# Layer kernel on one core: the SBUF buffers are declared in another order

## The chip, the cores and the metric

One core of a Trainium2 chip (trn2) runs the whole program. The metric is the device time of one execution in microseconds; a lower one is better. The profile is of a separate execution, with its own time.

## The reference, cut to what matters

The input x has 8 batches of 2048 rows of 256 numbers, all float32. For every row:

```python
xn = layernorm(x)                                  # no gain, no offset
q, k, v = split(xn @ Wqkv + bqkv)                  # 256 each
qp, kp = elu(q) + 1, elu(k) + 1
kv   = einsum('bsd,bse->bde', kp, v)               # per batch, over 2048 rows
attn = (qp @ kv) / (qp . sum(kp) + 1e-6)
z    = layer_norm(xn + attn) * g1 + b1
ffn  = (silu(z @ Wg + bg) * (z @ Wu + bu)) @ Wd + bd    # 682 hidden
s    = layer_norm(z + ffn) * g2 + b2
out  = x + s * silu(xn @ (ternary(weight) * scale).T)
```

## The kernel before, in words

The rows are cut into 32 groups of 512 (`GROUPS`, `TOK`), four groups to a batch. One iteration of the main loop works on several groups at once: the norm and keys of a group some steps ahead, the attention of the next one, the feed-forward part of the present one, the last norm of the one behind. In which order each engine takes its steps is written out by hand: `TENSOR_JOBS`, `SCALAR_STEPS`, `VECTOR_STEPS`, `GPSIMD_STEPS` for the steady iterations, `FILL_...` for the first and `END_...` for the last one. The engines meet at semaphores only.

Nearly all matmuls work on pairs of float32r parts. A factor is split into a high part (rounded, by ScalarE) and a low part (the rest, by VectorE), and `products` (L1271 holds the one call of `eng.matmul`) adds high·high, low·high and high·low. In a group of the profile the moving operand stands first and the stationary one second: `bank<-wk_h,xT_h` moves `wk_h` past a stationary tile of `xT_h`. The jobs by name, with their operands (moving, then stationary) and the columns moved:

- `G`, `U`, `GU`: gate and up projection, moving zT_h or zT_l, stationary wgu_h or wgu_l, 512 columns, 66 matmuls in an iteration
- `D`: down projection, moving wd_h or wd_l, stationary h_h, h_l or ht, 256 columns, 64 in an iteration
- `K`: keys, moving wk_h or wk_l, stationary xT_h or xT_l, 256 columns, 24
- `B`: the ternary product, moving tern, stationary xT_h or xT_l, 256 columns, 16
- `N`: numerators (and, in a 257th column, denominators), moving kv_h or kv_l, stationary qp_h or qp_l, 258 columns, 24
- `XK`: attention sums, keys times rows, moving kp_h or kp_l, stationary xn_h or xn_l, 256 columns, 24 (the first four groups use unsplit kp and xn or xq)
- `Q`: queries, moving xT_h or xT_l, stationary wq_h or wq_l, 512 columns, 12
- `KV`: once in a batch, moving wv_h or wv_l, stationary xk (which lies in kv_h and kv_l), 256 columns, 12

In program order every matmul is preceded by the load of its stationary tile, 128 columns, which the profile shows as LDWEIGHTS on its own row (PEld), beside the matmul before it.

Where a buffer lies is set by the order of the `sb(...)` calls in `build_kernel` and by nothing else: each buffer takes its bytes per partition, rounded up to 32, and the next one begins behind it. From the declared shapes this gives the places below (bytes in a partition, modulo 256), and from them how far the moving operand's place lies past the stationary one's. Columns, chunks and ring slots step by multiples of 256 bytes, except in kv_h, kv_l, qp_h and qp_l, where the second chunk lies 32 bytes further (their rows of 264 and 520 numbers); the difference is the same for both chunks.

| buffer | before | after |
|---|---|---|
| wd_h, wd_l | 32 | 160 |
| h_h, h_l, ht | 96 | 96 |
| kp_h, kp_l | 0 | 160 |
| xn_h, xn_l | 96 | 96 |
| wk_h, wk_l, tern | 64 | 224 |
| xT_h, xT_l, wq_h, wq_l | 96 | 96 |
| kv_h, kv_l | 32 | 224 |
| qp_h, qp_l | 96 | 96 |
| zT_h, zT_l, wgu_h, wgu_l | 96 | 96 |
| wv_h, wv_l | 96 | 192 |

| job | moving less stationary, before | after |
|---|---|---|
| G, U, GU, Q | 0 | 0 |
| D | 192 | 64 |
| XK | 160 | 64 |
| K, B | 224 | 128 |
| N | 192 | 128 |
| KV | 64, and 32 for its second chunk | 224, and 192 |

Of the kernel before, what the change touches and what calls it, by code (L numbers as in the profile page):

```python
# [30 lines left out]
P = 128  # L31
D = 256
DC = D // P
H = 682
HF = H // P
HT = H - HF * P
HC = HF + 1
# [6 lines left out]
TOK = 512  # L44
TILES = TOK // P
# [6 lines left out]
SHIFT = 8  # L52
# [9 lines left out]
LN0 = LEAD + 1  # L62
# [150 lines left out]
def build_kernel(nc, x, wqkv, bqkv, wg, bg, wu, bu, wd, bd, g1, b1, g2, b2, wt, out):  # L213
    f32, f32r = mybir.dt.float32, mybir.dt.float32r
# [9 lines left out]
    with ctx:  # L224
        def sb(name, shape, dt=f32):
            return ctx.enter_context(nc.sbuf_tensor(name, shape, dt))
# [2 lines left out]
            return ctx.enter_context(nc.semaphore(name))  # L229


        ident = sb("ident", [P, P])
        consts = sb("consts", [P, 4])
        masks = sb("masks", [P, 2])
        norm1 = sb("norm1", [P, 2, TILES])
        norm2 = sb("norm2", [P, 2, TILES])
        kp_h = sb("kp_h", [P, TILES, D], f32r)
        kp_l = sb("kp_l", [P, TILES, D], f32r)
        den = sb("den", [P, 2, 2])
        wd_h = sb("wd_h", [P, HC, D], f32r)  # L240
        wd_l = sb("wd_l", [P, HF, D], f32r)
        kv_h = sb("kv_h", [P, DC, D + SHIFT], f32r)
        hb = sb("hb", [P, 2 * HC])
        hb0 = sb("hb0", [P, 2 * HC])
        hb1 = sb("hb1", [P, 2 * HC])
        kv_l = sb("kv_l", [P, DC, D + SHIFT], f32r)
        ve = sb("ve", [P, 3, TILES])
        vecs = sb("vecs", [P, 5, DC])
        rstd0 = sb("rstd0", [P, LN0, TILES])
        wk_h = sb("wk_h", [P, DC, D], f32r)  # L250
        wk_l = sb("wk_l", [P, DC, D], f32r)
        tern = sb("tern", [P, DC, D], f32r)
        tscale = sb("tscale", [P, 4])
        wq_h = sb("wq_h", [P, DC, D], f32r)
        wq_l = sb("wq_l", [P, DC, D], f32r)
        xT_h = sb("xT_h", [P, XT, DC, TOK], f32r)
# [5 lines left out]
        zT_l = sb("zT_l", [P, DC, TOK], f32r)  # L262
        xn_h = sb("xn_h", [P, TILES, D], f32r)
        xn_l = sb("xn_l", [P, TILES, D], f32r)
        wv_h = sb("wv_h", [P, DC, D], f32r)
        wv_l = sb("wv_l", [P, DC, D], f32r)
        NGU = (2 * HF + 1) * P
        wgu_h = sb("wgu_h", [P, DC, NGU], f32r)
        wgu_l = sb("wgu_l", [P, DC, NGU], f32r)
        qp_h = sb("qp_h", [P, DC, TOK + SHIFT], f32r)  # L270
        nmr0 = sb("nmr0", [P, LN0, TILES])
        mv = sb("mv", [P, 3, TILES, 2])
        qp_l = sb("qp_l", [P, DC, TOK + SHIFT], f32r)
        st = sb("st", [P, 3, TILES, 6])
        bvb = sb("bvb", [P, D])
        bk1b = sb("bk1b", [P, D])
        g1b = sb("g1b", [P, D])
# [101 lines left out]

        bias_line = xq[:, 1:3, :, :].rearrange("p a t d -> p (a t d)")[0:1, 0:NGU]  # L380
        b1w = nc.dram_tensor("b1w", (NGU,), f32, kind="Internal").ap()
        turned = nc.dram_tensor("turned", (2, D, TOK), f32, kind="Internal").ap()
        z_turned = nc.dram_tensor("z_turned", (2, D, TOK), f32, kind="Internal").ap()
        ROW_PARTS = [slice(at, min(at + 512, NGU)) for at in range(0, NGU, 512)]

# [3 lines left out]
        xk_h, xk_l = kv_h[:, :, 0:D], kv_l[:, :, 0:D]  # L389
        raw_v = xq[:, 1:3, :, :].rearrange("p a t d -> p (a t d)")[:, NGU:NGU + DC * D].rearrange("p (c n) -> p c n", c=DC)  # L390

# [1088 lines left out]
```

## Time and profile before

| what | value |
|---|---|
| time, median of 3 runs | 1210.86 us (1210.26 to 1211.26) |
| time of the profiled execution | 1212.66 us |
| its span, first to last instruction | 1211.0 us |
| PE busy | 1190.9 us, 98% |
| DVE, ACT, POOL busy | 1082.2, 953.3, 841.7 us |

The span is the time from the first to the last instruction of the profiled execution; 1.7 us of that execution's time lie outside it. The profiled execution took 1.8 us more than the median of the runs. Matmuls overlap in the profile: one is listed with its whole duration, and the next starts well before that ends, so the time that a matmul costs is the distance from its start to the next start. The listed duration is longer by a nearly constant part.

### The profile page before, as it was taken

The numbers are of one execution on the slowest core, as the hardware profiler recorded it, in microseconds if no ns is written. First come the engines' busy times: TensorE is split into PE (matmuls) and PEld (weight loads), VectorE is DVE, ScalarE is ACT, GpSimd is POOL, SyncE is SP. The second block draws the span as 40 slices with busy tenths as digits, with TensorE's granted clock in tenths as the row PEclk, the third lists the DMA queues.
The fourth block names the chain that finished last, engine by engine and source line by source line (L and its number), as shares of the span: only waits on it lengthen the run. The fifth ranks groups of instructions, "written<-read, shape, count | busy, mean of one in ns | idle before, by whom it ended". The sixth has DMA issues, their size and how long they took to land.

```text
span 1211.0 us, 24021 instructions
## 1 busy us (share of the span) xinstructions
PE 1190.9 (98%) x7550; PEld 1070.2 (88%) x7550; DVE 1082.2 (89%) x2467; ACT 953.3 (79%) x1557; POOL 841.7 (70%) x994
## 2 busy tenths in 40 slices
PE   8999999999999999999999999999999999999997
PEld 6889998989988999989999988999988899888886
DVE  6988999999999999999999999999999999777765
ACT  7787888878888887888878888778797788867753
POOL 3443787767787776787767777667776677766676
PEclk9999999999999999999999999999999999999999
DMA  7213432334432334432234432234332343222201
GB/s 217 74 50 88 123 106 70 88 105 123 123 104 72 87 106 123 118 103 78 87 106 122 121 104 74 74 120 123 108 96 63 101 123 105 70 71 61 76 22 35
DMA packets 137524, 115.61 MB, mean 95 GB/s; under 512 B 12340, under 2 KB 122294, under 8 KB 137399
## 3 DMA queue, kind: packets, MB, share of 16 engines
q1 hardware_dynamic: 137398, 114.08, 32.2%
q8 instruction: 62, 1.02, 0.3%
q14 instruction: 64, 0.52, 0.1%
HBM read 67.38 MB, written 46.67 MB: 94 GB/s over the span
## 4 chain that ended last, share of the span: by engine, by line
PE 86%; DVE 7%; issue 2%; ACT 2%; DMA 1%; POOL 1%; SPq 0%; DVEq 0%; POOLq 0%; ACTq 0%
PE bank L1271 61%; PE d_bank L1271 17%; PE xk_bank L1271 7%; DVE st L922 1%; DMA z_turned<-xa 1%; DMA xa<-z_turned 1%; DVE rz L1054 1%; PE bank L1285 1%; DVE bank L1095 0%; DVE h_l L1105 0%; ACT rz L695 0%; DVE zT_l L1085 0%; POOL norm L569 0%; ACT hs L695 0%; DVE kp L1014 0%
## 5 line engine op out<-in xcount | busy, mean ns | idle before, releaser
L1271 PE MATMUL bank<-zT_h,wgu_h 128*128 128x512 f32 x704 | 275.6, 391 | 1.1 <-DVE rz L1054 1.0
L1271 PE MATMUL bank<-zT_l,wgu_h 128*128 128x512 f32 x704 | 275.7, 392 | 0.0
L1271 PE MATMUL bank<-zT_h,wgu_l 128*128 128x512 f32 x704 | 275.4, 391 | 0.0
L695 ACT ACTIVATE rz<-rz,norm 128x256 f32<-128x256 f32 x252 | 140.5, 596 | 57.7 <-DVE norm L1131 57.1
L569 POOL TENSOR_TENSOR norm<-ve,consts 128x4 f32<-128x4 f32 x64 | 72.9, 1139 | 153.6 <-DVE ve L933 153.5
L1271 PE MATMUL d_bank<-wd_h,h_h 128*128 128x256 f32 x640 | 179.2, 280 | 0.1
L1271 PE MATMUL d_bank<-wd_h,h_l 128*128 128x256 f32 x640 | 179.0, 280 | 0.0
L1271 PE MATMUL d_bank<-wd_l,h_h 128*128 128x256 f32 x640 | 179.0, 280 | 0.0
L1095 DVE SCALAR_TENSOR_TENSOR bank<-bank,hb,hs 128x512 f32<-128x512 f32 x160 | 117.9, 754 | 54.0 <-ACT hs L695 42.3
L695 ACT ACTIVATE h_h<-bank 128x512 fp32r<-128x512 f32 x160 | 95.8, 599 | 80.9 <-DVE bank L1095 80.5
L1271 PEld LDWEIGHTS bank<-zT_l,wgu_h 128*128 128x128 f32 x704 | 132.1, 188 | 28.8
L1271 PEld LDWEIGHTS bank<-zT_h,wgu_h 128*128 128x128 f32 x704 | 132.7, 189 | 25.8 <-DVE rz L1054 3.3
L695 ACT ACT_TABLE_LOAD x116 | 148.8, 1283 | 4.1 <-POOL wd_l L678 1.2
L1271 PEld LDWEIGHTS bank<-zT_h,wgu_l 128*128 128x128 f32 x704 | 132.2, 188 | 20.6
L695 ACT ACTIVATE hs<-bank,hb 128x512 f32<-128x512 f32 x192 | 128.3, 685 | 15.0 <-PE bank L1271 13.6
L592 POOL TENSOR_TENSOR ksum<-ksum,kp 128x256 f32<-128x256 f32 x120 | 106.9, 891 | 46.7 <-DVE kp L1021 43.3
L1105 DVE TENSOR_TENSOR h_l<-bank,h_h 128x512 fp32r<-128x512 f32 x160 | 110.0, 688 | 23.1 <-ACT h_h L695 17.4
L1271 PEld LDWEIGHTS d_bank<-wd_h,h_h 128*128 128x128 f32 x640 | 120.2, 188 | 3.1 <-DVE h_l L1105 0.5
L1271 PEld LDWEIGHTS d_bank<-wd_h,h_l 128*128 128x128 f32 x640 | 120.2, 188 | 2.7
L1271 PEld LDWEIGHTS d_bank<-wd_l,h_h 128*128 128x128 f32 x640 | 122.0, 191 | 0.0
L642 POOL TENSOR_TENSOR rz<-rz,g1b 128x256 f32<-128x256 f32 x128 | 118.0, 932 | 0.0
L602 POOL TENSOR_TENSOR rz<-rz,g2b 128x256 f32<-128x256 f32 x124 | 90.4, 739 | 35.0 <-ACT rz L695 35.0
(163 smaller groups left out, 3576.3 us busy)
## 6 DMA issues: line engine op xcount, KB each, us to landing
xq<-in_L_attn_x_dram SPq DMA_DIRECT2D x32, 512.0 KB, 6.0
xa<-in_L_attn_x_dram SPq DMA_DIRECT2D x31, 512.0 KB, 3.9
out_dram<-rz SPq DMA_DIRECT2D x31, 512.0 KB, 5.0
z_turned<-xa SPq DMA_DIRECT2D x120, 128.0 KB, 3.3
xa<-z_turned SPq DMA_DIRECT2D x30, 512.0 KB, 4.1
turned<-xa SPq DMA_DIRECT2D x108, 128.0 KB, 2.5
xa<-turned SPq DMA_DIRECT2D x27, 512.0 KB, 3.9
rz<-in_L_attn_Wg_dram SPq DMA_DIRECT2D x1, 640.0 KB, 5.2
```

The lines of the kernel that those rows point to most:

```text
L569: eng.tensor_tensor(dst, ve[:, k, :], neg_half[:, 0:1].to_broadcast([P, TILES]), ALU.pow).then_inc(S[f"rs{k}"], 1)
L592: eng.tensor_tensor(ksum[:, slot, :], ksum[:, slot, :], part, ALU.add).then_inc(S["ks"], 1)
L602: eng.tensor_tensor(row_, row_, g2b[:, :], ALU.mult).then_inc(S["a"], 1)
L642: eng.tensor_tensor(row_, row_, g1b[:, :], ALU.mult).then_inc(S["zg"], 1)
L695: return eng.activation(out_, in_, func, **kw).then_inc(S[name], 1)
L922: eng.bn_stats(st[:, k, t, :], rows).then_inc(S[f"bn{k}"], 1)
L1054: eng.scalar_tensor_tensor(out=rz[:, g % RZ, t, :], in0=num[:, 0:D], scalar=den[:, n % 2, 1:2], in1=rz[:, g % RZ, t, :], op0=ALU.mult, op1 ...
L1095: eng.scalar_tensor_tensor(out=hidden(g, c)[0:rows, :], in0=up, scalar=hb[0:rows, HC + c:HC + c + 1], in1=hs[0:rows, n % 2, :], op0=ALU.ad ...
L1105: eng.tensor_tensor(h_l[:, slot, :], hidden(g, c)[:, :], h_h[:, slot, :].bitcast(f32), ALU.subtract).then_inc(S["hl"], 1)
L1271: ins = eng.matmul(dst, left, right, start=first and n == 0, stop=last and n == len(pairs) - 1, **kw)
L1285: ins = eng.transpose(dst[:, c * D + t * P:c * D + (t + 1) * P], src[:, 2 * p + t, c * P:(c + 1) * P], ident[:, :])
```

## The change

Only the order of the `sb(...)` calls changes, and `NGU` is computed ahead of them. No shape, no instruction, no wait and no loop changes, and the whole set of buffers ends at the same place.

```diff
-        ident = sb("ident", [P, P])
+        NGU = (2 * HF + 1) * P
         consts = sb("consts", [P, 4])
-        masks = sb("masks", [P, 2])
-        norm1 = sb("norm1", [P, 2, TILES])
-        norm2 = sb("norm2", [P, 2, TILES])
         kp_h = sb("kp_h", [P, TILES, D], f32r)
         kp_l = sb("kp_l", [P, TILES, D], f32r)
-        den = sb("den", [P, 2, 2])
         wd_h = sb("wd_h", [P, HC, D], f32r)
         wd_l = sb("wd_l", [P, HF, D], f32r)
-        kv_h = sb("kv_h", [P, DC, D + SHIFT], f32r)
         hb = sb("hb", [P, 2 * HC])
-        hb0 = sb("hb0", [P, 2 * HC])
-        hb1 = sb("hb1", [P, 2 * HC])
-        kv_l = sb("kv_l", [P, DC, D + SHIFT], f32r)
-        ve = sb("ve", [P, 3, TILES])
-        vecs = sb("vecs", [P, 5, DC])
-        rstd0 = sb("rstd0", [P, LN0, TILES])
         wk_h = sb("wk_h", [P, DC, D], f32r)
         wk_l = sb("wk_l", [P, DC, D], f32r)
         tern = sb("tern", [P, DC, D], f32r)
-        tscale = sb("tscale", [P, 4])
+        masks = sb("masks", [P, 2])
+        rstd0 = sb("rstd0", [P, LN0, TILES])
         wq_h = sb("wq_h", [P, DC, D], f32r)
...
         xn_l = sb("xn_l", [P, TILES, D], f32r)
-        wv_h = sb("wv_h", [P, DC, D], f32r)
-        wv_l = sb("wv_l", [P, DC, D], f32r)
-        NGU = (2 * HF + 1) * P
         wgu_h = sb("wgu_h", [P, DC, NGU], f32r)
         wgu_l = sb("wgu_l", [P, DC, NGU], f32r)
         qp_h = sb("qp_h", [P, DC, TOK + SHIFT], f32r)
+        hb0 = sb("hb0", [P, 2 * HC])
+        kv_h = sb("kv_h", [P, DC, D + SHIFT], f32r)
+        hb1 = sb("hb1", [P, 2 * HC])
+        qp_l = sb("qp_l", [P, DC, TOK + SHIFT], f32r)
+        ve = sb("ve", [P, 3, TILES])
+        kv_l = sb("kv_l", [P, DC, D + SHIFT], f32r)
+        norm1 = sb("norm1", [P, 2, TILES])
+        norm2 = sb("norm2", [P, 2, TILES])
+        den = sb("den", [P, 2, 2])
+        vecs = sb("vecs", [P, 5, DC])
+        tscale = sb("tscale", [P, 4])
         nmr0 = sb("nmr0", [P, LN0, TILES])
         mv = sb("mv", [P, 3, TILES, 2])
-        qp_l = sb("qp_l", [P, DC, TOK + SHIFT], f32r)
         st = sb("st", [P, 3, TILES, 6])
+        ident = sb("ident", [P, P])
+        wv_h = sb("wv_h", [P, DC, D], f32r)
+        wv_l = sb("wv_l", [P, DC, D], f32r)
         bvb = sb("bvb", [P, D])
```

## Rows read from the trace of the kernel before

**Rows 1.** The page: busy time of each engine.
```profile
PE 1190.9 (98%) x7550; PEld 1070.2 (88%) x7550; DVE 1082.2 (89%) x2467; ACT 953.3 (79%) x1557; POOL 841.7 (70%) x994
```
**Rows 2.** Stretches of the span: length, busy us of each engine, granted clock, DMA.
```profile
100.00:1140.00 1040.00, 1037.36 (x6632) 937.90 (x6631) 954.85 (x2153) 842.04 (x1371) 751.67 (x873) 1.00 0.33 96
```
**Rows 3.** Chain of waits, 560 to 640 us: shares by line.
```profile
by line: PE bank L1271 73.6%; PE d_bank L1271 19.5%; PE xk_bank L1271 7.1%
```
**Rows 4.** PE's groups by shape, whole span: count, busy us, mean ns, idle before.
```profile
L1271 PE MATMUL bank<-zT_l,wgu_h 128*128 128x512 f32 x704 | 275.7, 392 | 0.0
...
L1271 PE MATMUL d_bank<-wd_h,h_l 128*128 128x256 f32 x640 | 179.0, 280 | 0.0
...
L1271 PE MATMUL bank<-kv_h,qp_l 128*128 128x258 f32 x256 | 72.9, 285 | 0.0
...
L1271 PE MATMUL bank<-wk_h,xT_l 128*128 128x256 f32 x256 | 72.0, 281 | 0.0
...
L1271 PE MATMUL bank<-tern,xT_h 128*128 128x256 f32 x256 | 63.3, 281 | 0.9 <-DVE tern L1210 0.9
...
L1271 PE MATMUL xk_bank<-kp_h,xn_l 128*128 128x256 f32 x224 | 63.1, 282 | 0.0
```
**Rows 5.** Timeline of PE: start us, length us; jobs D 0 and D 1.
```profile
565.46 0.28 PE L1271 MATMUL d_bank<-wd_h,h_h 128*128 128x256 f32 x1
...
566.04 0.28 PE L1271 MATMUL d_bank<-wd_l,h_h 128*128 128x256 f32 x1
...
568.19 0.39 PE L1271 MATMUL bank<-zT_h,wgu_h 128*128 128x512 f32 x1
```
**Rows 6.** PE's groups by shape, 566.0 to 568.15 us, inside D 0 and D 1.
```profile
L1271 PE MATMUL d_bank<-wd_h,h_h 128*128 128x256 f32 x7 | 1.9, 276 | 0.0
```
**Rows 7.** PE's groups by shape, 576.5 to 579.3 us, jobs D 2 and D 3.
```profile
L1271 PE MATMUL d_bank<-wd_h,h_h 128*128 128x256 f32 x8 | 2.2, 281 | 0.0
```
**Rows 8.** Timeline of PE: D 2 and D 3, then K 0, to the next job.
```profile
576.54 0.28 PE L1271 MATMUL d_bank<-wd_h,h_h 128*128 128x256 f32 x1
...
579.37 0.28 PE L1271 MATMUL bank<-wk_h,xT_h 128*128 128x256 f32 x1
...
580.79 0.28 PE L1271 MATMUL d_bank<-wd_h,h_h 128*128 128x256 f32 x1
```
**Rows 9.** Timeline of PE: the job N, four tiles, then G.
```profile
584.09 0.28 PE L1271 MATMUL bank<-kv_h,qp_h 128*128 128x258 f32 x1
...
587.00 0.40 PE L1271 MATMUL bank<-zT_h,wgu_h 128*128 128x512 f32 x1
```
**Rows 10.** PE's groups by shape, 589 to 593.7 us, gate and up, late in a row.
```profile
L1271 PE MATMUL bank<-zT_l,wgu_h 128*128 128x512 f32 x8 | 3.1, 389 | 0.0
```
**Rows 11.** PE's groups by shape, 564.0 to 565.4 us, one gate job behind B.
```profile
L1271 PE MATMUL bank<-zT_l,wgu_h 128*128 128x512 f32 x2 | 0.8, 397 | 0.0
L1271 PE MATMUL bank<-zT_h,wgu_l 128*128 128x512 f32 x2 | 0.8, 395 | 0.0
L1271 PE MATMUL bank<-zT_h,wgu_h 128*128 128x512 f32 x2 | 0.8, 392 | 0.0
```
**Rows 12.** Timeline of PE: the first chunk of a KV job.
```profile
617.98 0.28 PE L1271 MATMUL bank<-wv_h,kv_h 128*128 128x256 f32 x1
618.10 0.28 PE L1271 MATMUL bank<-wv_h,kv_l 128*128 128x256 f32 x1
618.22 0.28 PE L1271 MATMUL bank<-wv_l,kv_h 128*128 128x256 f32 x1
618.33 0.28 PE L1271 MATMUL bank<-wv_h,kv_h 128*128 128x256 f32 x1
```
**Rows 13.** PEld's groups by shape, 576.5 to 579.3 us, loads in D 2 and D 3.
```profile
L1271 PEld LDWEIGHTS d_bank<-wd_l,h_h 128*128 128x128 f32 x8 | 1.5, 192 | 0.0
L1271 PEld LDWEIGHTS d_bank<-wd_h,h_l 128*128 128x128 f32 x8 | 1.5, 188 | 0.0
```

## The prediction

> **What bounds the kernel now.** I read the page first. PE is busy for 98% of the span and no other engine comes near it except DVE with 89% [rows 1]. Then I cut the span into stretches: from 100 to 1140 us PE is busy for 1037.36 of 1040 us, DVE for 954.85, and the granted clock is 1.00, its level of 2.4 GHz [rows 2]. The chain of waits of two iterations consists of PE's lines alone [rows 3]. So in the steady part the time is the number of matmuls times the distance between their starts. The change leaves the number alone. It can act only through that distance, or through a handful of waits at the ends.
>
> The groups by shape say that this distance is not one number for one shape. Matmuls of 128x256 last 280 ns in the down projection, 281 in keys and ternary products, 282 in the attention sums; those of 258 columns last 285 [rows 4]. To turn a duration into a cost I compare it with starts. In D 0 and D 1 the sixth of 24 matmuls starts at 566.04 and the next job at 568.19, so 19 steps take 2.15 us, 113.2 ns each [rows 5], at a duration of 276 ns [rows 6]. D 2 and D 3, the same instructions on other chunks, take 24 steps in 2.83 us, 117.9 ns [rows 8], at 281 ns [rows 7]. The duration is the step plus 163 ns in both, so a difference of durations is a difference of cost. K 0 takes 1.42 us for 12, 118.3 ns a step [rows 8]; N takes 2.91 us for 24, 121.2 ns [rows 9]. Gate and up have two paces as well: 389 ns late in a row of such jobs [rows 10], 392 to 397 in the job behind B [rows 11].
>
> The fastest pace seen, 113.2 ns for 256 columns, I call the **floor**; it is 276 ns of duration, 389 for 512 columns, and by its 0.44 ns a column 277 for 258. Over the floor lie: down 4 ns x 2048 = 8.2 us; K, B and XK 5 ns x 1952 (768 + 512 + 672) = 9.8 us; N 8 ns x 768 = 6.1 us; gate, up and queries 2.5 ns x 2496 = 6.2 us [rows 4, 6, 10]. That is 30 us, 2.5% of the span, and all that places could give.
>
> **Why places may matter.** The weight load of the next matmul runs beside the present one, so two streams read SBUF at once. In D 2 and D 3 at the slow pace every third load lasts 192 ns and not 188 [rows 13]. The kinds of job that are seen at the floor, gate and up at difference 0 [rows 10] and D at 192 [rows 6], have differences that are multiples of 64. K at 224 is not at it [rows 8], and the means of B at 224 and XK at 160 lie 5 and 6 ns above [rows 4]. The pace has a memory: D 0 needs five steps, 0.58 us or 116 ns each, to come down to the floor [rows 5], D 2 behind a settled gate job never does [rows 7], and the gate job behind B needs six. So a job that settles helps the one behind it too.
>
> Against this speaks a rule of the Trainium skill, SBUF — State Buffer, "Who interferes with whom": the two read ports of PE, for the moving operand and for weights, are independent, and only the port pair shared by VectorE and GpSimd causes contention. By it the new order changes nothing. And the same skill, TensorE: Matmul & The Clock Gate, "Back-to-back issue gap", gives N/2.4 + 2.5 ns, which is 109 ns for 256 columns by that page, below every step in the trace; rows of one shape that differ by 5 ns do not fit either.
>
> **The change part by part.** It removes no instruction and adds none; no DMA, wait or queue is touched. What moves is the place of nearly every buffer that a matmul reads.
>
> 1. *K, B, XK* (1952 matmuls) go from differences with an odd 32 to 128, 128 and 64. No row shows 128. The nearest rows for 64 are the first chunk of KV: 617.98 to 618.33 us, three steps, 117 ns each [rows 12], between floor and today's pace. The gain lies between the whole 9.8 us (floor) and a loss: at the pace of N, 3 ns more, 1952 x 3 = 5.9 us. I take a third of the gain, what a kind gets that is at the floor for part of its steps, as D is: 1952 x 1.7 ns = 3.3 us less.
> 2. *What stands behind them.* A gate or up job behind B has durations that average (397 + 395 + 392)/3 = 394.7 ns, 5.7 over the floor, for 6 matmuls: 34 ns [rows 11]. The order of jobs has two gate or up jobs behind B in an iteration, two behind XK and one behind N, about 150 in all. At 34 ns each the upper end is 5 us; the lower end is nothing. If the job before ends settled, the entry still costs something; I take 1.5 us less.
> 3. *D* (2048) goes from 192 to 64. Bounds: all at the floor, 8.2 us less; all at 281 ns, 1 ns x 2048 = 2.0 us more; at N's pace of 285 on top, 10 us more. KV at 64 was seen only at 117 ns, in steps that are too few to settle [rows 12], which is D's mean now. I take 0.
> 4. *N* (768) goes from 192 to 128, but its chunks stay 32 bytes apart while it alternates between them every third matmul, so the stationary tile loaded across that edge is at an odd 32 whichever the order. Bounds 4 ns either way, 3 us; I take 0.
> 5. *G, U, Q* keep their difference of 0; *KV* (96 matmuls) goes from 64 and 32 to 224 and 192: 4 ns either way is 0.4 us; 0.
> 6. *Other engines.* Small vectors (norms, masks, den, biases) move as well. Their instructions lie under PE, with DVE at 92% of the steady stretch [rows 2], 85 us free. If that cover were gone, PE would wait at the steps of DVE; a PE that is faster by 1% still leaves DVE below 93%. Cost 0.
>
> Sum: -3.3 - 1.5 = -4.8 us. The profiled execution took 1212.66 us (span 1211.0 and 1.7 around it), so this gives 1207.9 for such an execution; the median lies 1.8 us lower, which gives **1206.0 us**.
>
> **The rivals.**
>
> *A. All multiples of 64 settle.* K, B, XK and D reach the floor for most of their steps, and the jobs behind them gain: 9.8 + about 5 of D's 8.2 + 2 = 17 us less, **1194 us**. For it: G and Q reach the floor for long rows [rows 10]. Against: D at 192, also a multiple, stays at 281 ns for whole jobs [rows 7].
>
> *B. Place does nothing, or the gains and losses cancel:* **1211 us**. The skill's rule of independent ports, named above, would give this. For it: the two paces of D occur at one and the same difference, so something other than the difference picks them. Against: no kind with an odd 32 has a mean as low as D's [rows 4]. In this case the durations of rows 4 come back unchanged.
>
> *C. Slower: 64 is a worse place for D.* D loses the floor it has in D 0 and D 1 and settles where each load of stationary h meets the moving wd. From 280 ns to 281 costs 2 us; to N's 285, 10 us. It decides when D's mean is above 282.4, since by then 2048 x 2.4 ns = 4.9 us have eaten the gain of parts 1 and 2. At 283 and with no gain in K, B and XK it gives 1211 + 6 = **1217 us**. For it: D is the only 256-column kind that is at the floor now, and it gives that place up; KV at 64 shows 117 ns and not 113. Against: three steps prove little.
>
> That the change does not do what it says I can exclude: the differences follow from the declared shapes.
>
> **How the numbers follow.** A measurement of this kernel tells 0.2%, 2.4 us, from no change. The forecast (a modest gain, 1201 to 1208.4) gets 0.41, A 0.16, B 0.18, C 0.25. So faster 0.57, same 0.18, slower 0.25. The range reaches into A down to 1194 and into C up to 1217; what lies outside is a full settling of N and gates too, or D at N's pace. The likeliest case's own range is 1201 to 1208.4.
>
> **What would show it.** Right: the groups wk, tern and xk at 278 to 280 ns where they had 281 and 282; a gate job behind B with durations nearer to 389 than 395; the count of matmuls unchanged and PE still at 98%. Step 3 is right if d_bank stays at 280. A shows as 276 or 277 in all 256-column groups. B shows as every group within 1 ns of before. C shows as d_bank at 283 or more, and loads of 192 ns in all D jobs. It would be wrong in kind if PE's groups kept their durations and the time moved anyway, by waits on DVE.

## The result and the profile after

The changed kernel takes 1212.87 us (median of 19 runs, 1211.62 to 1214.14) beside 1210.66 us for the kernel before on the same chip (19 runs): a ratio of 1.0019, 95% interval 1.0012 to 1.0025. It is slower by 2.2 us, inside the 0.2% that I had called no change but clear of the interval, where 4.8 us less was forecast. The ratios below each compare an order with the kernel before, run beside it on one chip (its median there was 1209.84, 1210.15 or 1211.03 us), and they leave out one slow run each of two orders, 3043 us with K and B alone at 128 and 2391 us with XK alone at 64.

The two profiled executions show almost the same span, 1210.9 us and 1211.0, so this difference can't be read from the spans: an execution scatters by 1 to 2 us, and the profiled one of the kernel before (1212.66 us) was slower than any of its 19 runs. It can be read from the steps, the distances from one matmul's start to the next. First the page of the changed kernel, engine shares (answers to [rows 1]) and its stretch from 100 to 1140 us (answers to [rows 2]; length, then busy us of PE, PEld, DVE, ACT, POOL, clock, DMA).

```profile
PE 1191.5 (98%) x7550; PEld 1072.3 (89%) x7550; DVE 1080.3 (89%) x2467; ACT 953.4 (79%) x1557; POOL 845.9 (70%) x994
...
100.00:1140.00 1040.00, 1037.95 (x6633) 940.38 (x6632) 952.39 (x2153) 842.19 (x1372) 756.23 (x873) 1.00 0.33 96
```

PE is as busy as before, at the full clock, with the same 7550 matmuls. Its groups by shape (answer to [rows 4]):

```profile
L1271 PE MATMUL bank<-zT_h,wgu_h 128*128 128x512 f32 x704 | 277.1, 394 | 0.9 <-DVE rz L1054 0.9
...
L1271 PE MATMUL d_bank<-wd_h,h_l 128*128 128x256 f32 x640 | 178.7, 279 | 0.0
...
L1271 PE MATMUL bank<-kv_h,qp_l 128*128 128x258 f32 x256 | 72.3, 282 | 0.0
...
L1271 PE MATMUL bank<-tern,xT_l 128*128 128x256 f32 x256 | 64.0, 283 | 0.0
...
L1271 PE MATMUL xk_bank<-kp_h,xn_l 128*128 128x256 f32 x224 | 62.7, 280 | 0.0
```

By these durations the numerators gained 3 ns in the group shown and 1 in the mean of their three groups, the attention sums 2, the ternary product lost 2, and the down projection is unchanged or 1 ns better. The last is misleading. The starts say something else (answers to [rows 5]; jobs B 1, G 3, D 0 and D 1, start and length in us):

```profile
563.48 0.28 PE L1271 MATMUL bank<-tern,xT_h 128*128 128x256 f32 x1
...
564.44 0.40 PE L1271 MATMUL bank<-zT_h,wgu_h 128*128 128x512 f32 x1
...
565.84 0.28 PE L1271 MATMUL d_bank<-wd_h,h_h 128*128 128x256 f32 x1
...
568.66 0.39 PE L1271 MATMUL bank<-zT_h,wgu_h 128*128 128x512 f32 x1
```

B takes 0.96 us for 8, 120 ns a step. D 0 and D 1 take 2.82 us for 24, 117.5 ns a step, where the kernel before took 2.73 with 113.2 ns once settled [rows 5]. At place 64 a matmul of 279 or 280 ns costs 117.8 ns; at 192 one of 281 did [rows 7, 8]. So durations compare costs within one place only, and from here on I go by starts.

I took the distance from each matmul's start to the next over the whole trace, and took off 113.33 ns for 256 columns, 114.2 for 258, 226.67 for 512 (the settled steps). What is left is the **excess**, in us, summed by the kind of job; a step over 22 ns above that is counted as a wait instead, with what it has too much. The 0.4 us of KV stand in the column "all" only. The last three columns say in how many iterations a D job ran at the floor: D 0 and 1 of 31, D 2 and 3 of 26 (those that stand behind GU and ahead of K), D 4 and 5 of 26 (behind K).

```
kernel                 D      K     B     XK    N     G,U,GU Q     all    waits   D0,1 D2,3 D4,5
before                 6.80   3.72  2.49  3.58  5.14  4.80   0.76  27.7   15.5    23   0    2
after                  9.11   4.09  2.96  3.20  4.59  6.04   0.72  31.1   12.3    0    0    0
control_same_places    6.73   3.74  2.50  3.60  5.12  4.83   0.79  27.7   13.8    26   0    0
d64_only               7.50   3.65  2.50  3.60  5.25  5.40   0.92  29.2   13.4    0    0    23
after_but_d192         2.84   4.12  2.91  3.20  4.65  5.35   1.07  24.6   15.4    25   26   26
kb128_only             5.40   4.41  2.92  3.58  4.67  4.66   0.93  27.0   13.7    25   0    26
xk64_only              3.94   3.62  2.50  3.20  5.14  5.03   0.82  24.7   14.0    26   26   0
n128_only              6.37   3.72  2.49  3.60  4.77  4.96   0.85  27.2   14.1    28   0    2
kbxk32_d192            8.57   2.70  1.92  2.37  4.55  3.81   0.69  25.0   15.4    3    0    3
all_32                 7.03   2.52  1.97  2.39  4.11  4.96   0.74  24.1   15.7    0    0    0
all_zero               13.07  4.91  2.93  4.04  5.49  5.74   0.31  37.0   11.3    0    0    0
d192_n32               2.63   4.22  2.90  3.20  4.32  5.66   1.06  24.5   15.3    28   26   26
```

The change costs 3.4 us of steps: D 2.3, the gate and up jobs 1.2, K and B 0.8, against 0.9 that XK and N gain. The gate and up jobs keep their own places, so they lose by what stands ahead of them: over its six steps such a job has 41 ns of excess behind B instead of 33, 27 instead of 22 behind XK, and 24 instead of 11 behind D.

Excess and waits together account for the time: subtracted from the time of the profiled execution they leave 1168.5 to 1169.8 us in all twelve orders. Some of the loss in steps comes back as shorter waits of PE (below). How much can't be taken from the first two rows: the waits of the kernel before are 1.7 us longer than those of control_same_places, which has the same places.

### The profile page after: what moved, and what is told of

It reads as the page before. It is cut to its first block, busy times and chain, and to the rows that moved or that the text cites. A ratio compares the mean times of both kernels' runs of the same rounds, so it can differ in the third digit from the quotient of the medians.

```text
span 1210.9 us, 24021 instructions
## 1 busy us (share of the span) xinstructions
PE 1191.5 (98%) x7550; PEld 1072.3 (89%) x7550; DVE 1080.3 (89%) x2467; ACT 953.4 (79%) x1557; POOL 845.9 (70%) x994
## 4 chain that ended last, share of the span: by engine, by line
PE 94%; DVE 3%; issue 1%; ACT 1%; DMA 1%; POOL 1%; SPq 0%; DVEq 0%; POOLq 0%; ACTq 0%
PE bank L1271 66%; PE d_bank L1271 19%; PE xk_bank L1271 8%; DVE st L922 1%; PE bank L1285 1%; DMA xa<-z_turned 0%; DVE rz L1054 0%; DMA z_turned<-xa 0%; ACT rz L695 0%; POOL norm L569 0%; DVE bank L1095 0%; DVE mv L929 0%; DVE rz L1140 0%; DVE den L1051 0%; DVE xn L974 0%
## 5 line engine op out<-in xcount | busy, mean ns | idle before, releaser
L569 POOL TENSOR_TENSOR norm<-ve,consts 128x4 f32<-128x4 f32 x64 | 73.0, 1140 | 152.7 <-DVE ve L933 152.6
L1095 DVE SCALAR_TENSOR_TENSOR bank<-bank,hb,hs 128x512 f32<-128x512 f32 x160 | 117.9, 754 | 53.6 <-ACT hs L695 41.7
L1271 PEld LDWEIGHTS bank<-zT_h,wgu_h 128*128 128x128 f32 x704 | 132.3, 188 | 24.1 <-DVE rz L1054 2.5
L592 POOL TENSOR_TENSOR ksum<-ksum,kp 128x256 f32<-128x256 f32 x120 | 109.8, 915 | 46.9 <-DVE kp L1021 43.6
```

Source lines behind the costliest of these rows:

```text
L569: eng.tensor_tensor(dst, ve[:, k, :], neg_half[:, 0:1].to_broadcast([P, TILES]), ALU.pow).then_inc(S[f"rs{k}"], 1)
L592: eng.tensor_tensor(ksum[:, slot, :], ksum[:, slot, :], part, ALU.add).then_inc(S["ks"], 1)
L1095: eng.scalar_tensor_tensor(out=hidden(g, c)[0:rows, :], in0=up, scalar=hb[0:rows, HC + c:HC + c + 1], in1=hs[0:rows, n % 2, :], op0=ALU.ad ...
L1271: ins = eng.matmul(dst, left, right, start=first and n == 0, stop=last and n == len(pairs) - 1, **kw)
```

## The experiments

All orders of the layer below use the same buffers; the small vectors fill the gaps, and only places modulo 256 of what matmuls read are controlled. Where a diff gives places and not code, it stands for a list of `sb` calls in another order. Every stationary operand except that of KV and the second chunk of N's lies at 96. wv_h and wv_l, which only the 96 matmuls of KV use, are not held fixed when others move. The theories were: **P**, the difference of places alone sets a kind's step; **H**, the job ahead sets it; and, from the first results on, **J**, both together. The **entry** of a job is what the job ahead leaves behind for it.

### Only matmuls, every place

```diff
+            run(bank[0], mw[0], 512, WARM)
+            for d in range(8):
+                run(bank[0], mw[0], 512, GATE)
+                run(bank[1], mv[d], 256, LONG)
+            for d in range(8):
+                run(bank[2], mv[0], 256, GATE)
+                run(bank[3], mw[d], 512, WIDE)
+            for d in ORDER:
+                ins = run(bank[1], mv[d], 256, LONG)
```

> This kernel leaves the layer out: it fills a stationary buffer and 16 moving ones (places 0, 32, ... 224 past the stationary one, modulo 256) and runs only matmuls, 48 of 256 columns in a row for each place behind six of 512 columns, then 24 of 512 columns for each place, then the 256-column blocks back to back in another order. Theory P (the difference of places sets the step): each moving buffer has a pace of its own, and mvc (64), where D went, has a longer step (117 to 118 ns) than mvg (192), where D was (113); the pace of a buffer is the same in the first and in the last section. Theory H (history sets it): the pace of one buffer differs between the first section (behind 512 columns) and the last (behind another block) by the same 4 to 5 ns. Theory N (other engines' accesses slow PE): with the other engines idle every place gives 113 ns.

The timeline of PE merges a block to one line: start, length to the end of its last matmul, count. mva lies 0 past the stationary tile, mvb 32, mvc 64 and so on to mvh, 224; the mw buffers likewise. A block's cost is the distance to the next block's start. First the section in which six matmuls of 512 columns stand ahead of each block, one block of 512 columns at 0 and one at 192, then the end of the last section.

```profile
16.35 5.92 PE L76 MATMUL bank<-mva,st 128*128 128x256 f32 x48
22.10 1.55 PE L76 MATMUL bank<-mwa,st 128*128 128x512 f32 x6
23.49 5.76 PE L76 MATMUL bank<-mvb,st 128*128 128x256 f32 x48
29.09 1.55 PE L76 MATMUL bank<-mwa,st 128*128 128x512 f32 x6
30.48 5.82 PE L76 MATMUL bank<-mvc,st 128*128 128x256 f32 x48
36.13 1.55 PE L76 MATMUL bank<-mwa,st 128*128 128x512 f32 x6
...
58.87 5.82 PE L76 MATMUL bank<-mvg,st 128*128 128x256 f32 x48
64.53 1.52 PE L76 MATMUL bank<-mwa,st 128*128 128x512 f32 x6
...
72.28 5.63 PE L76 MATMUL bank<-mwa,st 128*128 128x512 f32 x24
77.75 0.88 PE L76 MATMUL bank<-mva,st 128*128 128x256 f32 x6
...
110.04 5.77 PE L76 MATMUL bank<-mwg,st 128*128 128x512 f32 x24
115.64 0.87 PE L76 MATMUL bank<-mva,st 128*128 128x256 f32 x6
...
150.34 5.76 PE L76 MATMUL bank<-mvb,st 128*128 128x256 f32 x48
155.94 5.62 PE L76 MATMUL bank<-mvg,st 128*128 128x256 f32 x48
161.40 5.91 PE L76 MATMUL bank<-mvd,st 128*128 128x256 f32 x48
```

At 0 a block takes 5.75 us, 120 ns a step; at 32 5.60, 117; at 64 5.65, 118. At 192 it takes 5.66 us behind the 512-column matmuls and 5.46, 113.3 ns once settled, behind the block at 32: the same instructions at the same place, two paces. The settled steps of all places, behind 512 columns and in the last section:

```
place     0      32     64     96     128    160    192    224
behind    120.0  116.7  117.8  120.0  120.0  118.8  117.8  118.3
last      120.0  116.7  117.8  120    118.7  117.5  113.3  118.3
```

So theory P holds for 0, 32, 64, 96 and 224, H for 192 and, less, for 128 and 160. The other engines' compute is idle all this time, but copies to memory run for the first 54 us of the kernel. They are not the reason for the two paces at 192, whose slow block starts at 58.87 us, behind them; for 128 and 160 this kernel can't tell the entry from the copies. Theory N falls: with the other engines idle no place but one has 113 ns. With 512 columns only the place 0 settles at 226.7 ns a step; at 192 they take 5.60 us for 24, 233 ns.

### The same places in another order

```diff
-        ident = sb("ident", [P, P])
-        consts = sb("consts", [P, 4])
-        masks = sb("masks", [P, 2])
+        hb = sb("hb", [P, 2 * HC])
+        den = sb("den", [P, 2, 2])
+        norm1 = sb("norm1", [P, 2, TILES])
+        st = sb("st", [P, 3, TILES, 6])
+        kv_h = sb("kv_h", [P, DC, D + SHIFT], f32r)
...
```

> The buffers in yet another order, but with every operand of a matmul at the place modulo 256 that it has before the change (D 192, K and B 224, XK 160, N 192, gate and queries 0); only the small vectors and the places beyond 256 differ. Theory P (places modulo 256 decide): time within 0.1% of before (1210.7), D's durations with 276 and 281 as before. Theory F (something finer or coarser than modulo 256, or the small vectors' places, decides): time or D's pace moves by over 1 us.

1210.21 us, ratio 1.0004 (0.9994 to 1.0013), and an excess of 27.7 us as before, kind by kind within 0.07 us. Where a buffer lies beyond 256 bytes, and where the small vectors lie, makes no difference that shows. The control also shows what waits scatter by from one execution to another, 13.8 and 15.5 us.

### D alone at 64

```diff
-wd_h, wd_l at 32
+wd_h, wd_l at 160
```

> As the kernel before modulo 256, with D alone moved to 64 (wd at 160). Theory P: D loses the floor wherever it had it: +2.3 us of steps in D, and up to +1.2 us in the gate jobs behind it; time 1212.9 to 1214, as much as or more than the whole change. Theory H (D's fast pace came from the phase in which the job ahead left the stream, K, B, XK and N being the ones that changed it): D 0 and D 1 keep 113 ns in two of three iterations, time 1210.7.

1211.90 us, ratio 1.0016 (1.0007 to 1.0026): in time this is, within the noise, all of the loss of the whole change; in steps it is 1.5 us of the 3.4. D 0 and D 1 are at the floor in none of 31 iterations. But D as a whole lost only 0.7 us of steps, because D 4 and D 5, slow at 192, are at the floor at 64 behind K at 224. Timeline of PE, the start of D 2 and of the job behind D 3, then of D 4 and of the job behind D 5:

```profile
651.85 0.28 PE L1271 MATMUL d_bank<-wd_h,h_h 128*128 128x256 f32 x1
...
654.68 0.28 PE L1271 MATMUL bank<-wk_h,xT_h 128*128 128x256 f32 x1
...
656.10 0.28 PE L1271 MATMUL d_bank<-wd_h,h_h 128*128 128x256 f32 x1
...
657.91 0.28 PE L1271 MATMUL bank<-wk_h,xT_h 128*128 128x256 f32 x1
```

2.83 us for 24, 117.9 ns a step, and 1.81 us for 16, 113. Neither P nor H had this: a job at 64 can reach the floor as well, behind K.

### Everything at 0

```diff
-moving buffers at 0, 32, 64
+all moving buffers at 96, where all stationary ones are
```

> All matmul operands at place 96, so that every difference is 0. Gate jobs at 0 settle at 226.7 ns for 512 columns, which is the floor. Theory P with 0 as the good place: K, B, XK and D all at 113 to 115 ns, 15 us or more saved, about 1195. [...]

1217.06 us, ratio 1.0057 (1.0041 to 1.0074). Theory P's forecast of 1195 us had the wrong sign: the place that is best for 512 columns is, with 96, the worst for 256. D's excess is 13.1 us, 6.4 ns a step, as the matmul-only kernel has it at 0 (120.0 less 113.3 is 6.7).

### The changed kernel with D back at 192

```diff
-wd_h, wd_l at 160
+wd_h, wd_l at 32
```

> The places of the changed kernel (K, B, N 128, XK 64), with D alone back at 192. Theory P (D's own place decides whether it reaches 113.3 ns): D 0 and D 1 are at the floor again in some 23 of 31 iterations and the time is that of before, 1209.8, or 1 us less, for XK and N gained 0.9 us and K and B lost 0.8. Theory J (place and entry jointly: D reaches the floor only when the job ahead leaves the streams in the right phase): with B and XK at other places the gate job ahead of D ends elsewhere, D 0 and D 1 stay at 117.8 and the time stays at 1212 to 1213.

1209.36 us, ratio to before 0.9995 (0.9986 to 1.0004), where the changed kernel stands at 1.0019 (1.0012 to 1.0025). Moving one pair of buffers back removes the loss, and what is left is no measurable change. (KV goes from a difference of 224 to 0 in this order; its 96 matmuls have 0.4 us of excess in both.) D's excess is 2.84 us, not 9.11: all three pairs of D jobs run at the floor, D 2 and 3 and D 4 and 5 in every one of 26 iterations, which they never did before. Timeline, D 2 and D 3:

```profile
576.74 0.28 PE L1271 MATMUL d_bank<-wd_h,h_h 128*128 128x256 f32 x1
...
579.46 0.28 PE L1271 MATMUL bank<-wk_h,xT_h 128*128 128x256 f32 x1
```

2.72 us for 24. Both theories are too simple: P did not expect D 2 to 5, J expected D 0 and 1 to stay slow.

### K and B alone at 128, and XK alone at 64

```diff
-wk_h, wk_l, tern at 64
+wk_h, wk_l, tern at 224
```

> As the kernel before modulo 256, with wk and tern alone at 128. From the matmul-only kernel 128 costs 120 ns a step where 224 costs 118.3, if long enough; in the layer B rose by 0.9 ns and K by 0.5: +0.9 us in steps. Theory J: as B ends in another phase, D 0 and D 1, which keep their place 192, lose the floor, +1.5 to +2 us more, and D is at the floor in under 5 of 31 iterations: 1212.5. Theory P: D keeps it in 20 or more: 1210.7.

1210.3 us, ratio 1.0002 (0.9993 to 1.0012). K and B cost 1.1 us more, near the 0.9 expected, but D gains 1.4: D 0 and 1 keep the floor and D 4 and 5, which stand behind K, reach it in 26 of 26. Theory J's own forecast (D 0 and D 1 at the floor in under 5 iterations, 1212.5 us) was wrong, and P's time of 1210.7 was nearer. Yet D 4 and 5 show what P excludes: the place of K decides over D, which has not moved.

```diff
 qp_h
+kp_h
+kp_l
 hb0
 tscale
-kp_h
-kp_l
 norm2
```

> As the kernel before modulo 256, with kp alone at 64 from xn. Theory J: XK's own steps gain 0.4 us; GU stands behind XK and D 2 behind GU, so D 2 and D 3 (place 192, unchanged) go to the floor in 20 or more of 26 iterations, 24 x 4.4 ns x 26 = 2.7 us: 1207.5. Theory P: D 2 and D 3 stay at 117.8: 1209.8 to 1210.

1208.96 us, ratio 0.9979 (0.9970 to 0.9989). D 2 and D 3 are at the floor in 26 of 26 iterations, as J said beforehand, and D 0 and 1 and D 4 and 5 are as before. Steps: 24.7 us of excess, 3.0 less. D 2 and D 3 in the timeline take 2.73 us:

```profile
575.14 0.28 PE L1271 MATMUL d_bank<-wd_h,h_h 128*128 128x256 f32 x1
...
577.87 0.28 PE L1271 MATMUL bank<-wk_h,xT_h 128*128 128x256 f32 x1
```

The traces say more about the entry than the theories did. The last step of the gate or up job ahead of D is either 226 or 227 ns, which is settled, or 230 to 236, which is not. In the eight kernels that have D at 192, a D job of 24 matmuls behind a gate or up job reaches the floor in all 262 cases with the long last step and in none of the 194 with the settled one. The rows below are the gate matmul two places ahead of D and the first matmul of D: at D 0 and D 2 of the kernel before, then at D 2 with XK alone at 64. The two steps between them take 0.47, 0.45 and 0.46 us; the second of them is 236 ns (D at the floor), 227 (slow) and 233 (floor).

```profile
564.99 0.39 PE L1271 MATMUL bank<-zT_h,wgu_l 128*128 128x512 f32 x1
...
565.46 0.28 PE L1271 MATMUL d_bank<-wd_h,h_h 128*128 128x256 f32 x1
...
576.09 0.39 PE L1271 MATMUL bank<-zT_h,wgu_l 128*128 128x512 f32 x1
...
576.54 0.28 PE L1271 MATMUL d_bank<-wd_h,h_h 128*128 128x256 f32 x1
```

```profile
574.68 0.39 PE L1271 MATMUL bank<-zT_h,wgu_l 128*128 128x512 f32 x1
...
575.14 0.28 PE L1271 MATMUL d_bank<-wd_h,h_h 128*128 128x256 f32 x1
```

So at 192 it is the gate job that has *not* settled behind which D settles. At 64 this doesn't help: in the changed kernel 55 of 57 such gate jobs end long, and no D job behind one reaches the floor. The relation was found in the traces afterwards; no run set the last step on purpose.

### N alone at 128

```diff
-kv_h, kv_l at 32
+kv_h, kv_l at 224
```

> As the kernel before modulo 256, with kv_h and kv_l alone at 128 from qp. N's steps 0.5 us shorter, as in the changed kernel; no D job stands behind N, so D 0 and D 1 stay at the floor in some 23 of 31 and the others slow: 1209.7 (0 to -0.7 us). If D changes its share, the phase is carried further than one job.

1210.75 us, ratio 0.9997 (0.9988 to 1.0006). N's steps gain 0.4 us (0.55 in the changed kernel), and D 0 and D 1 are at the floor in 28 of 31 instead of 23 (26 in control_same_places, with nothing moved). That is 0.5 us of steps in all, too little for the time to show.

### Places at 32

```diff
-kp 0, wk and tern 64 (K, B, XK at 224, 224, 160)
+kp, wk and tern at 128 (K, B, XK at 32)
```

> K, B and XK at 32, D and N left at 192. In the matmul-only kernel 32 had 116.7 ns behind either kind of job, the lowest of all places that do not depend on the entry, and D's block at 192 directly behind a block at 32 went to 113.3. Theory J: K, B and XK gain 1.7 ns x 1952 = 3.3 us, and D 4, which stands behind K, goes to the floor, up to 4.4 ns x 900 = 4 us: 1203 to 1207. Rival: the short jobs (4 to 12 matmuls between changes of the stationary tile) are all transient, and nothing is gained in them: 1209 to 1212.

1208.29 us, ratio 0.9988 (0.9979 to 0.9997), outside the 1203 to 1207 of theory J. K, B and XK gain 2.8 us of steps, near the 3.3 expected, and gate and up 1.0. D behind them loses the floor (3 of 31) and 1.8 us. The expectation that D 4 would reach it, taken from one entry in the matmul-only kernel, was wrong (3 of 26): the entry is not the place of the job ahead alone. The gate jobs ahead of D end settled here in 54 of 57 cases, and D is slow behind each of those.

```diff
-wd 32, kv 32
+wd, kv at 128, with kp, wk and tern at 128
```

> D, K, B, XK and N all at 32. By the matmul-only kernel every 256-column step is 116.7 ns: D as before (mean 116.7), K, B and XK 1.7 ns less (3.3 us), N unknown: 1205 to 1208. Rival: gate jobs behind them lose more (24 ns a job behind 32 against 0 to 13 behind 192), 66 jobs behind D 0.7 us: 1209.

1208.41 us, ratio 0.9986 (0.9977 to 0.9994), between the 1205 to 1208 expected and the rival's 1209. D never settles at 113, and its excess is 3.4 ns a step, the 116.7 of place 32 whatever stands ahead. This order does not depend on entries.

### Only matmuls, every entry

```diff
+            for target in (6, 2):
+                for d in range(8):
+                    run(bank[2], mv[d], 256, ENTRY)
+                    run(bank[1], mv[target], 256, LONG)
+            for target in (6, 2):
+                for d in range(8):
+                    run(bank[2], mv[d], 256, ENTRY)
+                    run(bank[0], mw[0], 512, GATE)
+                    run(bank[1], mv[target], 256, LONG)
+            for d in range(8):
+                run(bank[2], mw[0], 512, GATE)
+                ins = run(bank[3], mv[d], 256, LONG, 64)
```

> Leaves the layer out, only matmuls: 24 of 256 columns at 192 (mvg) and at 64 (mvc), each behind 12 at every one of the eight places, once directly and once with six of 512 columns between; then 24 at each place with a stationary tile of 64 columns and not 128. Theory J (place and entry together): mvg settles at 113.3 ns behind some entries and at 117.8 behind others; behind 128 (mve) it settles at the floor, behind 224 (mvh) not; mvc settles at the floor behind fewer entries than mvg. Theory L (the excess is the weight load's reads meeting the moving reads): with a load half as long the step at 0 falls from 120 to 117 ns or less and most places come within 2 ns of 113.3. Rival to L: the load's length does not matter, 120 ns stays at 0.

The timeline, blocks merged: mvg (192) directly behind mve (128) and behind mvh (224); mvg behind mvc (64) with six gate-like matmuls between, and behind mvd (96) with them; two blocks with a load of 64 columns, at 0 and at 192.

```profile
33.32 2.91 PE L73 MATMUL bank<-mvg,st 128*128 128x256 f32 x24
...
45.95 2.99 PE L73 MATMUL bank<-mvg,st 128*128 128x256 f32 x24
...
95.37 1.55 PE L73 MATMUL bank<-mwa,st 128*128 128x512 f32 x6
96.76 2.89 PE L73 MATMUL bank<-mvg,st 128*128 128x256 f32 x24
...
100.91 1.53 PE L73 MATMUL bank<-mwa,st 128*128 128x512 f32 x6
102.28 2.99 PE L73 MATMUL bank<-mvg,st 128*128 128x256 f32 x24
...
173.92 2.89 PE L73 MATMUL bank<-mva,st 128*64 128x256 f32 x24
...
199.04 3.01 PE L73 MATMUL bank<-mvg,st 128*64 128x256 f32 x24
```

A block of 2.89 to 2.91 us has settled at 113.3 ns, one of 2.99 runs at 117.8. At 192 the block settles directly behind 0, 32, 64, 96 and 128 and stays slow behind 160, 192 (slow itself) and 224. With six 512-column matmuls between, it settles behind 64 and 128 only, so the entry is carried through a whole gate-like job. Behind these two the sixth step of the gate-like job is 233 and 236 ns, behind the other six places 226 or 227, as in the layer. At 64 all 16 blocks run at 117.8. That is theory J, with 192 as the place that has two paces here. It is not the only such place in the layer: D 4 and D 5 of d64_only reached the floor at 64 behind K at 224, and here 64 behind 224 is slow, so this kernel does not have every entry that the layer has. Theory L got half an answer: with stationary tiles of 64 columns and not 128 the step at 0 falls from 120 to 113.3 ns, but the one block at 192 runs at 119 and the others at 116 to 119. The narrower tile shortens the load and also halves the rows of the result, so that it is the load's reads that count is suggested and not shown, and a shorter load does not remove the excess in general.

### D at 192, N at 32

```diff
-kv_h, kv_l at 224, wd at 160
+kv_h, kv_l at 128, wd at 32
```

> The changed kernel's places with D back at 192 and N at 32. D at the floor for some 70% of its steps as with D at 192 before; N 0.5 us less than there (it had 4.1 us of excess at 32, 4.65 at 128). Steps: 24.1 us of excess against 27.7 before the change. If nothing of it came back as waits: 1206.2; with half of it back in the waits of Q for h_l, as seen so far: 1208. Ratio to before 0.997 to 0.9985.

1209.33 us, ratio 0.9982 (0.9971 to 0.9993), with 24.5 us of excess where 24.1 was expected, and a ratio inside the expected range.

## Why the prediction was wrong

**The step that failed is the reading in "Why places may matter" that a difference which is a multiple of 64 lets a job settle, and that "a job that settles helps the one behind it too".** The terms of parts 1 to 3 rest on it. In steps, part 1 (-3.3 us) measured +0.5, part 2 (-1.5) +1.2, and part 3, "*D* (2048) goes from 192 to 64 ... I take 0", +2.3. Part 1 is thus the largest miss, and part 3 the largest cost of the change: D 0 and D 1 lost the floor in all of their iterations, and the experiment that puts D back takes the changed kernel from 1.0019 to 0.9995.

The first half of the rule came from two kinds that settle at the floor, at 0 (512 columns) and at 192. The matmul-only kernel shows that it is no rule: with 256 columns 0 has 120 ns, 64 has 117.8, 128 has 118.7 or 120, and 192 has 113.3 only behind some entries. The second half has the wrong sign where it can be read best: D at 192 reaches the floor behind gate jobs that end unsettled, and behind settled ones never. The rows that the prediction rested on had it already, with D 0 fast behind the slow gate job of [rows 11] and D 2 slow behind a settled one [rows 7].

Rival C had the mechanism for D, giving up the one good place, but its price was too high: 117.8 ns a step is 4.5 over the floor for the steps that had it, 1.1 ns in D's mean, where I had put 3 ns more in the mean, 6 us. It also decided earlier than I said, since the gain that it had to eat was not there.

The yardstick failed as well. "A difference of durations is a difference of cost" held for the two paces at 192, from which it was taken, and not across places: D's durations fell by 0.3 ns in the mean while its steps grew by 1.1. By the signs that I had set, d_bank at 280 would have called step 3 right. (A slip without weight: the sum gives 1206.1 us, not 1206.0.)

*Part 1, K, B and XK.* Forecast -3.3 us; XK gained 0.4, K and B lost 0.8. The three steps of KV at 64, 117 ns [rows 12], were nearly right for 64, which settles at 117.8; for 128 there was no row, and it is no better than 224.

*Part 2, the jobs behind.* Forecast -1.5 us; gate and up cost 1.2 more. That one job sets the pace of the next was right, and moving XK alone changed D 2 and D 3 in every iteration.

*Part 4, N.* Taken as 0, it gained 0.55 us in steps.

*Part 6, other engines.* "Cost 0" was wrong in a way that the total hides. Where steps get shorter, waits mostly get longer: the changed kernel has 31.1 us of excess and 12.3 of waits, the one with D back at 192 24.6 and 15.4, the one with all at 0 37.0 and 11.3. A straight line through the twelve rows of the table gives 0.3 us more waits for each us of excess that goes, and a time that moves by 0.7 us for each us of excess. A single pair says little: waits of equal places differ by 1.7 us, and with XK alone at 64 only 0.2 us of 3.0 came back. Among the waits are those of the loads for the queries, for VectorE's h_l: PEld's waits of the changed kernel and of the one with D at 192 (us in total, times, longest):

```profile
PEld bank L1271 <- DVE h_l L1105: 2.6, 9, 0.3
```

```profile
PEld bank L1271 <- DVE h_l L1105: 5.5, 22, 0.5
```

The job Q 1 reuses a bank that h_low has to free. VectorE has 85 us free over the stretch, but not there. Waits seem to disturb the entry too: in the seven orders with D at 192 except kbxk32_d192, D 0 reaches the floor in 121 of 132 iterations with no wait of PE in the 21 steps ahead of it and in 60 of 85 with one.

*Rival A* (1194 us) fails with the rule of the multiples of 64: no group of 256 columns came to 276 or 277 ns.

*Rival B.* The rule of the Trainium skill, SBUF — State Buffer, "Who interferes with whom", is that the two read ports of PE are independent and only the port pair of VectorE and GpSimd causes contention. That did not make the order of buffers free: with all other engines idle the step of one instruction goes from 113.3 to 120 ns with the place of the moving operand alone. Whether the two ports contend, or something else depends on the place, no run shows. The formula N/2.4 + 2.5 of the Trainium skill, TensorE: Matmul & The Clock Gate, "Back-to-back issue gap", 109 ns for 256 columns, is given there for an isolated matmul and not for a stream of loads and matmuls; the settled steps of these float32r streams do not reach it, with 113.3 ns as the best. In size, though, B was nearest: it said 1211 us, and 1212.9 was measured.

The chances were set too far towards a gain: 0.57 for faster rested on one inference from two kinds of job. That the measured time lies between rivals B and C and so inside the wide range is no merit of the forecast.

A version that beats both kernels came out: XK alone moved to 64, 0.9979 of the time before, 2.5 us less. Orders with everything at 32, or with D at 192 and N at 32, gain about as much within their intervals. It is the best of ten orders, each measured in one session, so its 2.5 us is likelier too large than too small. Of the 27.7 us of excess no order removed more than 3.6.

What stays open is why an entry acts as it does, and what in the reads makes a place slow. The places of stationary operands other than 96 were not tried on purpose, so these runs show an effect of the moving operand's place, and that the difference to the stationary one is what counts is only suggested. KV gives a hint for it: with wv left at 96, the second and third steps of the job take 116.5 to 117.0 ns with its stationary kv at 32 (six orders) and 118.0 at 224 (n128_only), 119.0 at 96 (all_zero, where D ahead of it moved too). Another order of jobs was not tried either.

## What to carry to other kernels

When PE is the bound and its starts are 3 to 6% further apart than the best seen in the same trace, the place of the moving operand modulo 256 bytes, with that of the stationary one held fixed, is worth an experiment of a few lines: a kernel of matmuls alone that runs each place, behind each neighbour, gives most of the table in one run. Compare starts, not durations, and don't extend a good place from one width of matmul to another. Test a set of moves one at a time, and then together: here XK's move alone gave 0.9979, N's and that of K and B no change, D's a loss (1.0016), and the three without D 0.9995, since one job's place sets the pace of another.

## What was not expected of the hardware

- With the moving operand 192 bytes (modulo 256) past the stationary one, a row of float32r matmuls of 256 columns has two stable paces, 113.3 and 117.8 ns, and which one it takes is decided by the job ahead, even through six matmuls of 512 columns. Behind a gate job the fast pace goes with a last gate step of 230 to 236 ns (262 of 262) and the slow one with 226 or 227 (194 of 194).
- With 512 columns, place 0 settles at 226.7 ns and the other seven at 232 to 234; with 256 columns places 0 and 96 are the worst, 120 ns.
- With stationary tiles of 64 columns and not 128 the step at place 0 goes from 120 to 113.3 ns, and the one block at 192 runs at 119.
- The listed duration of a matmul exceeds its step by 163 ns at 192 and by 162 at 64, enough to hide a difference of 1 ns in 2048 matmuls.
